# A bilinear feature kernel on one core: W in thirteen pieces, part 0's loads and the tail units spread over the chunks

## The reference

```python
def _L0_rec_ref(feature, weight):          # (512, 200, 64), (200, 64, 64)
    bilinear = jnp.einsum('bie,ied->bid', feature, weight)
    out = jnp.einsum('bid,bjd->bij', bilinear, feature)
    return out                             # (512, 200, 200)
```

## Time and profile before

| | |
|---|---|
| median of 3 runs | 316.3 us (315.22 to 317.37) |
| the profiled execution's own time | 315.12 us |
| its span, first to last instruction | 313.3 us |
| mean granted TensorE clock | 0.95 |
| TensorE busy | 238.1 us (76%) |
| data queue's packets | 92.3% of 16 DMA engines |

### The profile page before, as it was taken

The page is one execution under the profiler, slowest core; times in us unless marked ns, Lnnn a source line. Parts: engine busy times, 40 slices in busy tenths (PEclk is TensorE's granted clock), DMA queues, the critical chain, the costliest instruction groups (busy, mean ns, idle before and its releaser), DMA issues.

```text
span 313.3 us, 14575 instructions
## 1 busy us (share of the span) xinstructions
PE 238.1 (76%) x6784; PEld 210.7 (67%) x6784; DVE 151.0 (48%) x176; ACT 128.0 (41%) x177; POOL 2.0 (1%) x5
## 2 busy tenths in 40 slices
PE   0076776999986976799869776999875775999950
PEld 0074676978876866677668675977875775978940
DVE  0033534636772763536546455445565455736640
ACT  1022334444553444244535344344454453544630
POOL 2000000000000000000000000000000000000000
PEclk9996879899997999999988999799999999999995
DMA  7999999798999999998899999988899999677996
GB/s 249 428 410 443 403 409 377 248 371 342 341 381 408 415 410 411 420 368 322 328 386 394 415 414 405 367 349 320 332 353 401 413 411 391 242 311 298 378 411 285
DMA packets 25708, 115.63 MB, mean 369 GB/s; under 512 B 4272, under 2 KB 4272, under 8 KB 25264
## 3 DMA queue, kind: packets, MB, share of 16 engines
q1 hardware_dynamic: 25648, 114.71, 92.3%
HBM read 32.77 MB, written 81.92 MB: 366 GB/s over the span
## 4 chain that ended last, share of the span: by engine, by line
PE 76%; issue 14%; DMA 4%; SPq 1%; DVE 1%; ACT 0%
PE psum L253 49%; PE psum L224 17%; PE psum L270 8%; DMA w_sb<-w_dram 4%; SPq L136 1%; PE psum L236 1%; DVE tile L285 1%; ACT mixed L306 0%
## 5 line engine op out<-in xcount | busy, mean ns | idle before, releaser
L253 PE MATMUL psum<-x_sb,mixed 64*64 64x200 f32 x3072 | 169.2, 355 | 22.3 <-issue 20.1
L253 PEld LDWEIGHTS psum<-x_sb,mixed 64*64 64x64 f32 x3072 | 136.9, 141 | 38.9 <-issue 27.4
L285 DVE COPY tile<-psum 128x800 f32<-128x800 f32 x100 | 99.2, 992 | 102.2 <-PE psum L253 92.9
L285 ACT COPY tile<-psum 128x800 f32<-128x800 f32 x100 | 82.6, 827 | 82.0 <-PE psum L253 63.8
L224 PE MATMUL psum<-x_sb,w_sb 64*64 64x64 f32 x3072 | 65.5, 227 | 39.1 <-issue 21.7
L224 PEld LDWEIGHTS psum<-x_sb,w_sb 64*64 64x64 f32 x3072 | 64.0, 140 | 42.2 <-issue 40.8
L306 DVE COPY mixed<-psum 64x512 f32<-64x512 f32 x48 | 33.1, 689 | 29.1 <-PE psum L224 27.9
L306 ACT COPY mixed<-psum 64x512 f32<-64x512 f32 x48 | 27.8, 580 | 40.8 <-PE psum L224 40.2
L308 ACT COPY mixed<-psum 128x512 f32<-128x512 f32 x24 | 14.1, 587 | 48.5 <-PE psum L224 48.5
L270 PE MATMUL psum<-x_sb,tails 128*32 128x200 f32 x512 | 25.2, 343 | 0.2 <-issue 0.2
L308 DVE COPY mixed<-psum 128x512 f32<-128x512 f32 x24 | 16.6, 690 | 17.4 <-PE psum L224 17.4
## 6 DMA issues: line engine op xcount, KB each, us to landing
out_dram<-tile SPq DMA_DIRECT2D x192, 400.0 KB, 5.6
x_sb<-x_dram SPq DMA_DIRECT2D x64, 400.0 KB, 7.1
w_sb<-w_dram SPq DMA_DIRECT2D x2, 2048.0 KB, 16.3
out_tail_dram<-tile SPq DMA_DIRECT2D x8, 400.0 KB, 3.6
w_sb<-w_dram SPq DMA_DIRECT2D x1, 2304.0 KB, 21.2
```

Of the source, the lines that this page charges most:

```text
L253: last = nc.tensor.matmul(psum[half_rows(pair), n % BANK_PAIRS * 2 + h, a * FIELDS:(a + 1) * FIELDS], mixed[half_rows(h), (CHUNKS * g + c) ...
L285: copy(tile[:, k % SLOTS, engine], psum[:, bank:bank + 2, 0:2 * FIELDS]).then_inc(copied[engine], 1)
```

## The change

W comes in 13 transfers: 12 of 16 fields (512 KB, 4,096 bytes a partition), one for each mix unit, and one for the 8 tail fields. They are issued in the order in which the units use them, among the loads of part 1. In group 0 each mix unit waits for its own piece.

Part 0 is still loaded in 8 transfers of 400 KB, now each for 8 quads and every other partition: 64 partitions of 6,400 bytes. For the next group they are issued behind tiles 1, 3, 5 and 7 of chunk 0 and tiles 1, 2, 4 and 5 of chunk 1, one behind each.

The first tail unit stands after tile 4 of chunk 1, the second after tile 2 of chunk 2. Each is stored by itself, as one transfer of 128 partitions by 3,200 bytes, and takes a slot of its own (`stored` counts what a slot's stores have added).

```diff
-PART0_LOADS = 8
+PART0_AFTER = ((0, 1), (0, 3), (0, 5), (0, 7), (1, 1), (1, 2), (1, 4), (1, 5))
+PART0_LOADS = len(PART0_AFTER)
...
-TAIL_AFTER = (2, 4)
+TAIL_AFTER = ((1, 4), (2, 2))
...
-STRIP_STORES = STRIPS * 16
-W_PIECES = ((0, CHUNK), (CHUNK, 2 * CHUNK), (2 * CHUNK, FIELDS))
+W_PIECES = FIELDS // MIX_FIELDS + 1
+TAIL_PIECE = W_PIECES - 1
...
-                if c == 1 and t in TAIL_AFTER:
-                    tail(n, g, TAIL_AFTER.index(t))
+                if (c, t) in TAIL_AFTER:
+                    tail(n, g, TAIL_AFTER.index((c, t)))
...
+def stored(k):
+    return sum(16 * (STRIPS if OUT_TILES[i][0] == "score" else 1) for i in range(k % SLOTS, k, SLOTS))
...
     def load_part0(eng, g, n):
-        size = QUADS // PART0_LOADS
-        quads = slice(n * size, (n + 1) * size)
-        eng.dma_start(x_sb[:, 2 * (g % 2), quads], x[g, 0, :, quads]).then_inc(part0_loaded[g % 2], 16)
+        size = QUADS * STRIPS // PART0_LOADS
+        quads, i = slice(n // STRIPS * size, (n // STRIPS + 1) * size), n % STRIPS
+        eng.dma_start(x_sb[i::STRIPS, 2 * (g % 2), quads], x[g, 0, i::STRIPS, quads]).then_inc(
+            part0_loaded[g % 2], 16)
...
             for n in range(PART0_LOADS):
                 load_part0(sp, 0, n)
-            load_w(0)
+            for n in range(MIX_UNITS):
+                load_w(n)
             for p in range(PIECES):
                 load_part1(sp, 0, p)
-            load_w(1)
-            load_w(2)
+                if p in MIX_AFTER:
+                    load_w(MIX_UNITS + MIX_AFTER.index(p))
+            load_w(TAIL_PIECE)
+            for n in range(2 * MIX_UNITS, TAIL_PIECE):
+                load_w(n)
...
+                if kind == "tail":
+                    e, = rest
+                    sp.wait_ge(copied[e], COPIES[NUMBER["tail", g, e]][e])
+                    sp.dma_start(out_tail[g, :, e], tile[:, k % SLOTS, e]).then_inc(done, 16)
...
-                    if c == 0:
-                        load_part0(sp, g + 1, t)
+                    if (c, t) in PART0_AFTER:
+                        load_part0(sp, g + 1, PART0_AFTER.index((c, t)))
...
-                if g == 0 and m == 0:
-                    pe.wait_ge(w_loaded[c], 16)
+                if g == 0:
+                    pe.wait_ge(w_loaded[c * MIX_UNITS + m], 16)
...
-                    eng.wait_ge(slot_out[k % SLOTS], STRIP_STORES * (k // SLOTS))
+                    eng.wait_ge(slot_out[k % SLOTS], stored(k))
```

More of the change, by code:

```diff
@@ L95, in tail @@
         add(n, e == 0, e == 1, ((e,), (e,)), "tail", g, e)
-        if e == 1:
-            tiles.append(("tail", g))
+        tiles.append(("tail", g, e))
     def mix(n, g, c, m):
@@ L125, in build @@
     zeroed = sem("zeroed")
-    w_loaded = [sem(f"w_loaded{n}") for n in range(len(W_PIECES))]
+    w_loaded = [sem(f"w_loaded{n}") for n in range(W_PIECES)]
     part0_loaded = [sem(f"part0_loaded{b}") for b in range(2)]
@@ L146, in load_w @@
             def load_w(n):
-                a, b = W_PIECES[n]
-                sp.dma_start(w_sb[:, a:b, :], weight[:, a:b, :]).then_inc(w_loaded[n], 16)
+                fields = slice(n * MIX_FIELDS, min((n + 1) * MIX_FIELDS, FIELDS))
+                sp.dma_start(w_sb[:, fields, :], weight[:, fields, :]).then_inc(w_loaded[n], 16)
             for n in range(PART0_LOADS):
                 load_part0(sp, 0, n)
-            load_w(0)
+            for n in range(MIX_UNITS):
+                load_w(n)
@@ L153, in _ @@
             for p in range(PIECES):
                 load_part1(sp, 0, p)
-            load_w(1)
-            load_w(2)
-            for k, (kind, g, *rest) in enumerate(OUT_TILES):
[L158 to L163, removed]
+                if p in MIX_AFTER:
+                    load_w(MIX_UNITS + MIX_AFTER.index(p))
@@ new lines, in _ @@
+            load_w(TAIL_PIECE)
+            for n in range(2 * MIX_UNITS, TAIL_PIECE):
+                load_w(n)
+            for k, (kind, g, *rest) in enumerate(OUT_TILES):
+                done = slot_out[k % SLOTS]
+                if kind == "tail":
+                    e, = rest
+                    sp.wait_ge(copied[e], COPIES[NUMBER["tail", g, e]][e])
+                    sp.dma_start(out_tail[g, :, e], tile[:, k % SLOTS, e]).then_inc(done, 16)
+                else:
+                    for e in range(2):
+                        sp.wait_ge(copied[e], COPIES[NUMBER["score", g, *rest, e]][e])
+                    to = out[g, rest[0], rest[1]]
+                    for i in range(STRIPS):
+                        sp.dma_start(to[i::STRIPS], tile[i::STRIPS, k % SLOTS]).then_inc(done, 16)
@@ L164, in _ @@
                 if kind == "score" and g + 1 < GROUPS:
                     c, t = rest
-                    if c == 0:
-                        load_part0(sp, g + 1, t)
+                    if (c, t) in PART0_AFTER:
+                        load_part0(sp, g + 1, PART0_AFTER.index((c, t)))
                     if c == CHUNKS - 1:
                         load_part1(sp, g + 1, t)
-            for s in range(SLOTS):
-                sp.wait_ge(slot_out[s], STRIP_STORES * len(range(s, len(OUT_TILES), SLOTS)))
+            for k in range(len(OUT_TILES), len(OUT_TILES) + SLOTS):
+                sp.wait_ge(slot_out[k % SLOTS], stored(k))
@@ L232, in tail_mix @@
                 if g == 0:
-                    pe.wait_ge(w_loaded[CHUNKS - 1], 16)
+                    pe.wait_ge(w_loaded[TAIL_PIECE], 16)
                 for r in range(TAIL):
@@ L294, in tail @@
                     eng.wait_ge(unit_ready, n + 1)
-                    copy_tile(n, TILE_OF["tail", g])
+                    copy_tile(n, TILE_OF["tail", g, e])
             def mix(n, g, c, m):
```

## The result

The changed kernel takes 321.69 us (median of 4 runs, 320.33 to 322.44) against 315.89 for the kernel before beside it. The ratio is 1.017, with an interval of 1.012 to 1.023: slower by 1.2 to 2.3%. (Some executions of any kernel here run a few per cent slower than its others; ratios and their intervals leave those out, the medians shown don't.) Forecast was 304.5. Rival B, which had 6% and came to 323.1, is nearest to what happened.

The account below looks back on a forecast made before the run. DMA was taken as first limit, with holes where TensorE's code blocks arrive late. Span 313.3 - 4.7 (group 0) - 7.0 (groups 1, 2) - 1.6 (group 3) + 1.5 (wait) = 301.5, median 304.5 us; range 298.5 to 312.5.

Parts of the forecast that it names:

- Rival B: Groups: code blocks stay at 5.7 us throughout, as no light stage is left; 323.1 us, chance 0.06.
- The budget's first half: Per group: 27.25 MB, 65.8 us at 414 GB/s, and 3392 TensorE instructions, 13.25 blocks, divided by chunk.
- the price of a block: Groups 1 and 2: 4.95 us a block in chunks 0 and 1, 5.6 in chunk 2; 68.5 us a group.
- the bound, 75.5 a group: Groups 1 and 2: every block at 5.7 us, a loss of 3.5 us a group.
- The argument against B: Groups: DMA would then run below full, and there blocks took 4.6 us.
- The start: Mix unit 0 waits for less of W: 3.7 us earlier, first matmul near 13.6, first store 27.4.
- Sum 4.7: Group 0: start 3.7 us earlier, plus 1.0 from shorter blocks in chunk 0, nothing from chunks 1 and 2.
- The hole at 55 to 59: Group 0: DMA falls to 161 GB/s at mean clock 0.76; forecast to stay after the change.
- Group 3: One tail unit moves from chunk 1 to chunk 2 and hides in the backlog: gain 1.6 us (0 to 2.5).
- Packets: Changed packet sizes of part 0, tail stores and W: together 0 (+-1) us.
- The tight wait: Next group's mix unit 0 waits for part 0's last load: 0.5 us a group, 1.5 in all (0 to 9).
- Rival A: Groups 1 and 2: code no limit once stages are even, DMA alone sets 65.8 us; 297.6 us, chance 0.13.

Follow-up runs that it names:

- W's change alone: Kernel before with only W in 13 pieces and each tail unit stored by itself: 313.91 us, ratio 0.985; on another chip 313.46, 0.988.
- The cut kernels: Kernel before, changed kernel, and changed kernel with earlier part 0 loads, each with 400-column score matmuls (half the scores wrong): 301.60, 301.64, 301.60 us.

## Why the prediction was wrong

The budget's first half held: the blocks of 256 instructions, their count per chunk, the bytes per chunk. The step that failed is the price of a block: "I take 4.95 there (between 4.6 and 5.1, nearer 5.1)". In group 1 the four blocks from 104.79 to 127.90, in chunk 0, took 5.78 us each, and the four from 127.90 to 151.34, in chunk 1, 5.86 (the first of these four is the one that the lower clock sets); the mean over 42 is 5.68. The 4.6 us row was from a store-only stretch, the 5.1 row from one without loads as well, as group 3 has none. Neither had loads under way, which is what the change puts in chunk 1 and leaves in chunk 0. The stage with loads had 6.2 us in the earlier trace rows and 5.7 on the mean, and the bound, 75.5 a group, was worked out from it; groups took 76.4 and 77.9. Halving chunk 0's loads did not shorten its blocks: three from 107.39 to 124.25 had taken 5.62 each before. Chunk 2's 5.6 us a block, 25.2 us, was more than the 23.7 and 24.1 measured; the miss of 8 and 9 us a group lies in chunks 0 and 1.

The argument against B, "DMA would then run below full, and there blocks took 4.6", failed on the same point. Below full and with loads they take 5.6. That B's total of 320.1 us of span is so near the 320.7 measured is in part luck. It had +7.0 for groups 1 and 2, -1.2 up to group 1's first store and +1 for group 3; measured were +10.0, +0.6 and -3.1.

The clock had no term beyond the new wait's. TensorE was busy 4.8 us longer with the same matmuls. How much of that reached the end was not tested: W's change alone has 241.3 us busy in its trace, near the changed kernel's 242.9, and a span of 312.7.

The start: as forecast (13.60, first store at 27.51), and SP kept ahead. Group 0's "Sum 4.7" failed: the lead at group 1's first store was gone. The hole at 55 to 59 did not stay, it came earlier: at 50 to 54 DMA moves 191 GB/s at a mean clock of 0.53, after 3.4 us of pause that ended at 48.24. Group 0 took 77.2 us instead of 73.0. With the old load places the same start is worth 1.2 to 1.5% (W's change alone).

Group 3: 3.1 us were gained between its first store and the end, where I had 1.6.

Packets: forecast zero, and putting part 0's rows back shows no effect outside the intervals.

The tight wait: forecast 0.5 a group, none in the profile, where TensorE is late itself. It appears at up to 7.3 us when the code is shortened, so the term was mis-sized in both directions. With the loads at their old places and the same shortened code waits for x reach 3.8 us as well.

Rival A's premise was that without the code's limit the evened stages pay. The cut kernels gave 301.6 with even and with uneven stages, with DMA's packets at 95.5 to 96.1% of the span in all of them. So with less code the uneven stages had left DMA next to no holes to fill, and evening them won nothing.

The Trainium skill (Runtime: NRT & Kernel Launch, Instruction fetch mechanics) has block crossings "mostly hidden". The runs go against it in this kernel: with the number of crossings cut by 23% the time fell by 4.8 and 6.4%.

## What to carry to other kernels

Where an engine runs through a long unrolled program, look for pauses on "issue" in the middle of a unit, count the instructions between them, and treat the arrival of code as a stage of its own. Where the trace has an instruction queue, see whether each pause ends a fixed time after one of its packets. Price the block from a row with the same kind of traffic that the change will put beside it, loads or stores, not only the same rate. A stage that looks idle for DMA can be the one in which the code catches up; filling it can cost more than the hole.

## What was not expected of the hardware

A block of TensorE's code took 4.70 us on the mean with stores alone and 5.68 with loads in every chunk, at 341 and 361 GB/s over the whole run. Even with 76 MB instead of 116 it stayed at 4.90. Its own transfer is short (0.9 to 1.0 us); most of the delay passes before it starts. Why loads weigh more than stores was not shown.

DMA can be fully busy and slow, as in this window of the changed kernel:

```profile
135.00:140.00 5.00, 3.61 (x120) 3.15 (x113) 2.56 (x3) 2.17 (x5) 0.00 (x0) 1.00 1.02 335
```

In windows of 2 us between 40 and 300, 11 of the 94 with a share of 0.95 or more were under 370 GB/s in the changed kernel, and 6 of 98 before. Over the whole run the data queue's packets took 294.7 us for 289.2, for the same bytes, so 5.5 of the 7.4 us are packets that took longer, and only 1.9 more are DMA with nothing to do. With the loads back in chunk 0 the packets took 289.3 us, and with the code cut 288.3. So, with stores in these strips, slower packets came only where loads stand in chunk 1 and TensorE is late as well; which of the two makes the other was not shown. That the loads' places cost 2.4% holds either way.
